# Turning the sums over the keys in blocks of 32 by 32 on VectorE

## The reference

```python
scores = jnp.clip(jnp.einsum('bhqd,bhkd->bhqk', Q, K), -80.0, 80.0)     # Q, K: 8 + 4 rotary dimensions
scores = jnp.where(causal, scores, -jnp.inf)
weights = jax.nn.softmax(scores / jnp.sqrt(jnp.float32(d_qk)), axis=-1)  # d_qk = 12
attn = jnp.einsum('bhqk,bhkd->bhqd', weights, V)
attn = attn.transpose(0, 2, 1, 3).reshape(B, S, N_HEADS * D_H)
x = _layernorm(x + attn @ W_O, axis=-1)
```

## Time and profile before

| | |
|---|---|
| time, median of 3 runs | 467.28 us (465.78 to 469.02) |
| time of the profiled execution | 468.31 us |
| its span | 466.6 us |
| mean granted TensorE clock | 0.978 |

### The profile page before, as it was taken

How to read it: one execution, slowest core, us unless ns; L and a number is a source line. 1 busy time by engine, 2 the same in 40 slices (tenths; PEclk the granted TensorE clock), 3 DMA queues, 4 the chain that set the end, 5 groups by cost and what they waited for, 6 DMA issues and landing times. The chain is left out here.

```text
span 466.6 us, 12398 instructions
## 1 busy us (share of the span) xinstructions
PE 430.2 (92%) x4259; PEld 233.6 (50%) x4259; DVE 370.6 (79%) x838; ACT 348.1 (75%) x548; POOL 166.9 (36%) x165
## 2 busy tenths in 40 slices
PE   7899999999999999999999999997999899699980
PEld 5543443434344344344443443443444798599970
DVE  4598789989896988989799889999888388366670
ACT  0697887988779888887988988787987554466650
POOL 8112112106315211431512115322002566688882
PEclk9999999999999999999999999998999899899995
DMA  3746647845442570156118305443410356577710
GB/s 100 193 124 147 156 122 152 205 128 126 102 94 68 131 162 6 42 119 138 46 35 187 77 1 136 91 99 89 115 25 1 93 145 165 156 185 212 196 55 6
DMA packets 33181, 51.67 MB, mean 111 GB/s; under 512 B 5675, under 2 KB 16337, under 8 KB 33120
## 3 DMA queue, kind: packets, MB, share of 16 engines
q1 hardware_dynamic: 25504, 37.04, 34.0%
q10 hardware_dynamic: 5344, 9.57, 7.3%
q0 software_dynamic: 2272, 4.27, 2.7%
HBM read 20.82 MB, written 5.33 MB: 56 GB/s over the span
## 5 line engine op out<-in xcount | busy, mean ns | idle before, releaser
L950 ACT ACTIVATE prob<-ring 128x1024 f32<-128x1024 f32 x288 | 273.9, 1036 | 44.9 <-PE ring L1096 43.7
L1114 PE MATMUL o_acc<-prob,v_stat 128*32 128x512 f32 (+3 forms) x1536 | 154.5, 497 | 3.2 <-DVE prob L626 2.5
L1096 PE MATMUL ring<-queries,keys 32*128 32x512 f32 (+3 forms) x1536 | 122.5, 382 | 0.9 <-ACT prob L950 0.9
L1096 PEld LDWEIGHTS ring<-queries,keys 32*128 32x128 f32 x1536 | 66.5, 184 | 72.8 <-issue 43.2
L519 POOL CAST parts<-whole_kq 128x512 fp32r<-128x512 f32 x32 | 39.1, 1221 | 139.0 <-DVE whole_kq L594 139.0
L626 DVE SCALAR_TENSOR_TENSOR prob<-prob,mask_hi 128x1024 f32<-128x1024 f32 (+1 forms) x80 | 86.1, 1076 | 0.0
L612 DVE TENSOR_SCALAR prob<-prob 128x2048 f32<-128x2048 f32 x64 | 77.4, 1220 | 7.2 <-ACT prob L950 6.2
L1023 ACT ACTIVATE prob<-ring,b1T 128x128 f32<-128x128 f32 x156 | 44.5, 368 | 38.0 <-PE ring L1214 16.8
L625 DVE TENSOR_SCALAR prob<-prob 128x1024 f32<-128x1024 f32 (+1 forms) x80 | 63.4, 793 | 11.8 <-ACT prob L950 11.6
L527 POOL DMA_INDIRECT by_expert<-xrow,index x32 | 42.9, 1341 | 50.9 <-DVE index L721 43.1
L1114 PEld LDWEIGHTS o_acc<-prob,v_stat 128*32 128x32 f32 x1536 | 34.1, 109 | 51.2 <-issue 34.0
(11 more groups left out here) (106 smaller groups left out, 312.7 us busy)
## 6 DMA issues: line engine op xcount, KB each, us to landing
queries<-parts SPq DMA_DIRECT2D x62, 256.0 KB, 3.9
v_stat<-in_w ACTq DMA_DIRECT2D x34, 256.0 KB
keys<-parts SPq DMA_DIRECT2D x64, 128.0 KB, 2.4
queries<-by_expert SPq DMA_DIRECT2D x39, 66.0 KB
xrow<-in_x_rows SPq DMA_DIRECT2D x8, 264.0 KB, 4.2
xT<-in_x_T SPq DMA_DIRECT2D x8, 256.0 KB
v_stat<-in_w SPq DMA_DIRECT2D x5, 256.0 KB
out<-prob,queries POOLq DMA_INDIRECT x39
```

Source lines behind the costliest of these rows:

```text
L950: act.activation(prob[u % P_SLOTS][:, 2 * half:2 * half + 2, :].rearrange("p h s -> p (h s)"), slot(u, half)[:], ACT.Exp, scale=SCALE).the ...
L1096: last = pe.matmul(out[:, j % 2 * QC + off:j % 2 * QC + off + w], keys[hg][r, kt * P:(kt + 1) * P], queries[hg][r, qc, part, QC - w:QC], s ...
L1114: last = pe.matmul(o_acc[j * VW:(j + 1) * VW, QC - w:QC], v_stat[b % 2][:, hg, kt, j, :], prob[u % P_SLOTS][:, j, off:off + w], start=begi ...
```

## The change

The sums are turned on VectorE by an instruction that transposes each 32x32 block of a [128, 512] tile where it stands. Since a head's rows lie in one group of 32 partitions, the turned block has queries in partitions, and 32 columns for each run of 32 queries: 9 of one group, 9 of the other, and the rest unused. `turn_sum` reads `o_acc` itself and its end (`o_turned`) lets TensorE begin the next sum; `normalize` makes one reciprocal and one product for both groups, and behind the second pair turns the result back the same way, straight into `flipped`. The jobs `turn` and `flip`, and ScalarE's copies for them, are gone. The rows of W_O are reordered on the way in to match. The other jobs move: two projections from steps 2 and 25 to 3 and 26, one from 20 to 21, `out` from 29 to 27 and from 7 to 4, `turnx`, `gate`, `rank` from 33, 34, 35 to 31, 32, 33 and from 11, 12, 13 to 9, 11, 12. In the tail every late job stands one tile sooner.

```diff
-OWN_JOBS = {0: ("project", 2, 0), 2: ("project", 3, 0), 6: ("project", 2, 1), 8: ("project", 3, 1),
-            9: ("turn", 0, 0), 22: ("turn", 0, 1), 26: ("turn", 1, 0), 28: ("flip", 0), 29: ("out", 0),
-            33: ("turnx", 0), 34: ("gate", 0), 35: ("rank", 0)}
-LATE_JOBS = {4: ("turn", 1, 1), 5: ("flip", 1), 7: ("out", 1), 11: ("turnx", 1), 12: ("gate", 1), 13: ("rank", 1)}
+OWN_JOBS = {0: ("project", 2, 0), 3: ("project", 3, 0), 6: ("project", 2, 1), 8: ("project", 3, 1),
+            27: ("out", 0), 31: ("turnx", 0), 32: ("gate", 0), 33: ("rank", 0)}
+LATE_JOBS = {4: ("out", 1), 9: ("turnx", 1), 11: ("gate", 1), 12: ("rank", 1)}
 NEXT_JOBS = {10: ("latent", 0), 14: ("latent", 1), 15: ("v", 0), 16: ("v", 1), 18: ("project", 0, 0),
-             20: ("project", 1, 0), 23: ("project", 0, 1), 25: ("project", 1, 1)}
+             21: ("project", 1, 0), 23: ("project", 0, 1), 26: ("project", 1, 1)}
...
-TAIL_AT = {1: "turn", 2: "flip", 3: "out", 6: "turnx", 7: "gate", 8: "rank"}
-PLAN_AT = (8, 9, 10)
+TAIL_AT = {2: "out", 5: "turnx", 6: "gate", 7: "rank"}
+PLAN_AT = (7, 8, 9)
...
+            def turn_sum(k):
+
+
+                dve.wait_ge(weighted, last_unit(k) + 1)
+                dve.transpose(o_blocks[k % 2][:], o_acc[:]).then_inc(o_turned, 1)
+
             def normalize(k):
 
                 pair, qc = k // NQC % PAIRS, k % NQC
-                dve.wait_ge(turned, k + 1)
-                o = misc[:].rearrange("p (t h c) -> p t h c", h=HG, c=VW)
-                inverse = rsum[:].rearrange("p (g t h) -> p g t h", g=2, h=HG)
-                for g in range(2):
-                    last = dve.reciprocal(inverse[:, g], o[:, :, :, g * VS + DH])
-                last.then_inc(rsum_ready, 1)
+                o = o_blocks[k % 2][:].rearrange("p (n r) -> p n r", r=VW)
+                dve.wait_ge(o_turned, k + 1)
+                dve.reciprocal(rsum[:], o[:, :, DH:2 * VS:VS]).then_inc(rsum_ready, 1)
                 dve.wait_ge(rsum_ready, k + 1)
...
+                rows = attn_blocks[qc][:].rearrange("p (n r) -> p n r", r=VW)[:, :, pair * 2 * DH:(pair + 1) * 2 * DH]
+                dve.tensor_tensor(rows.rearrange("p n (g d) -> p n g d", d=DH),
+                                  o[:, :, 0:2 * VS].rearrange("p n (g c) -> p n g c", c=VS)[:, :, :, 0:DH],
+                                  rsum[:].unsqueeze(3).to_broadcast([P, QC // VW, 2, DH]), ALU.mult).then_inc(attn_ready, 1)
+                if pair == PAIRS - 1:
+                    dve.wait_ge(attn_ready, k + 1)
+                    dve.transpose(flipped[qc][:], attn_blocks[qc][:]).then_inc(attn_turned, 1)
...
             for u in range(B * UB):
                 if job_at(u // UB, u % UB):
                     before_clip(*job_at(u // UB, u % UB))
+                if sum_ended(u) is not None:
+                    turn_sum(sum_ended(u))
                 clip(u)
+                if sum_ended(u) is not None:
+                    normalize(sum_ended(u))
...
             for c in range(TILES + 2):
                 if c < TILES:
                     residual(c)
+                if c == 0:
+                    turn_sum(sums(B - 1, 1, 1))
+                    normalize(sums(B - 1, 1, 1))
...
-            def o_evac(k):
-
-                act.wait_ge(weighted, last_unit(k) + 1)
-                if k >= 2:
-                    act.wait_ge(turned, k - 1)
-                act.activation(o_sb[k % 2][:], o_acc[:], ACT.Copy).then_inc(o_out, 1)
...
-                        pe.wait_ge(o_out, k)
+                        pe.wait_ge(o_turned, k)
...
-                if kind == "turn":
-                    pe.wait_ge(o_out, i + 1)
-                    pe.wait_ge(ident_ready, 2)
-                    for t in range(QC // P):
-                        last = pe.transpose(misc[:, t * P:(t + 1) * P], o_sb[i % 2][:, t * P:(t + 1) * P], ident[:])
-                    last.then_inc(turned, 1)
-                elif kind == "flip":
-
-                    pe.wait_ge(attn_ready, sums(i // Q, 1, q) + 1)
-                    for t in range(QT):
-                        last = pe.transpose(misc[:, t * P:(t + 1) * P], attn[:, q * QT + t, :], ident[:])
-                    last.then_inc(flip_mm, 1)
-                elif kind == "out":
-                    pe.wait_ge(flip_out, i + 1)
+                if kind == "out":
+                    pe.wait_ge(attn_turned, i + 1)
...
+    rows = a["L0_attn_W_O"].reshape(PAIRS, 2, HG, DH, D).transpose(2, 0, 1, 3, 4)
+    return np.ascontiguousarray(rows.reshape(HEADS * DH, D))
```

More of the change, by code:

```diff
@@ L94, in numbered @@
     kind, *which = job
-    if kind == "turn":
-        return kind, sums(b, *which)
     return (kind, b, *which) if kind == "project" else (kind, b * NQC + which[0])
@@ L131 @@
 TAIL_JOBS = [numbered(LATE_JOBS[n], B - 1) for n in sorted(LATE_JOBS)]
-TAIL_AT = {1: "turn", 2: "flip", 3: "out", 6: "turnx", 7: "gate", 8: "rank"}
-PLAN_AT = (8, 9, 10)
+TAIL_AT = {2: "out", 5: "turnx", 6: "gate", 7: "rank"}
+PLAN_AT = (7, 8, 9)
 EARLY_PLAN_AT = (B - 1) * UB + 16
-ROUTE_AT = {9: (0, 1), 10: (2, 3)}
-PAD_AT = 9
+ROUTE_AT = {8: (0, 1), 9: (2, 3)}
+PAD_AT = 8
 PADS_ACT = 2
@@ L218, in build @@
         prob = [sb(f"prob{i}", [P, HG, QC]) for i in range(P_SLOTS)]
-        o_sb = [sb(f"o_sb{i}", [P, QC]) for i in range(2)]
-        rsum = sb("rsum", [P, 2 * QC // P * HG])
-        attn = sb("attn", [P, NKT, D])
+        o_blocks = [sb(f"o_blocks{i}", [P, QC]) for i in range(2)]
+        rsum = sb("rsum", [P, QC // VW, 2])
+        attn_blocks = [sb(f"attn_blocks{i}", [P, QC]) for i in range(NQC)]
         xrow = [sb(f"xrow{i}", [P, QT, ROW]) for i in range(Q)]
@@ L300, in build @@
         scored, exped, clipped, weighted = sem("scored"), sem("exped"), sem("clipped"), sem("weighted")
-        o_out, turned, rsum_ready, attn_ready = sem("o_out"), sem("turned"), sem("rsum_ready"), sem("attn_ready")
-        flip_mm, flip_out, out_mm = sem("flip_mm"), sem("flip_out"), sem("out_mm")
+        o_turned, rsum_ready, attn_ready = sem("o_turned"), sem("rsum_ready"), sem("attn_ready")
+        attn_turned, out_mm = sem("attn_turned"), sem("out_mm")
         x_rows_in = [sem(f"x_rows_in{i}") for i in range(Q)]
@@ L336, in taken @@
             i = which[0]
-            return {"turn": (attn_ready, i + 1), "flip": (flip_out, i + 1), "out": (added, i + 1),
+            return {"out": (added, i + 1),
                     "turnx": (turnx_out, i + 1), "gate": (logits_out, i + 1), "rank": (carried, i + 2),
@@ L354, in sums_of, with sum_ended @@
             return sums(u // UB, u // NU % PAIRS, UNITS[u % NU][0])
+        def sum_ended(u):
+            return sums_of(u - LAG) if u >= LAG and last_unit(sums_of(u - LAG)) == u - LAG else None
         def last_unit(k):
@@ L723, in job @@
             def job(kind, i):
-                if kind == "turn":
-                    normalize(i)
                 if kind == "out":
@@ L742, in before_clip @@
                     turn_queries(*which)
-                if kind == "turn":
-                    normalize(*which)
                 if kind == "out":
@@ L974, in job @@
                     v_evac(i)
-                if kind == "flip":
-                    act.wait_ge(flip_mm, i + 1)
-                    act.activation(flipped[i % Q][:], misc[:], ACT.Copy).then_inc(flip_out, 1)
                 if kind == "turnx":
@@ L990, in _ @@
                 exp(u, 1)
-                if u >= LAG and last_unit(sums_of(u - LAG)) == u - LAG:
-                    o_evac(sums_of(u - LAG))
                 if job_at(u // UB, u % UB):
@@ L1032, in _ @@
                 relu(c)
-                if c == 0:
-                    o_evac(sums(B - 1, 1, 1))
                 if c + 2 < TILES:
@@ L1150, in job @@
                     pe.wait_ge(normed, i + 1)
+                    pe.wait_ge(ident_ready, 2)
                     for t in range(QT):
@@ L1299, in key_query_weights, with output_weights @@
     return out
+def output_weights(a):
+    rows = a["L0_attn_W_O"].reshape(PAIRS, 2, HG, DH, D).transpose(2, 0, 1, 3, 4)
+    return np.ascontiguousarray(rows.reshape(HEADS * DH, D))
 def constants():
@@ L1339 @@
         "w_latent": latent_weights(a), "w_kq": key_query_weights(a), "W_UV": a["L0_attn_W_UV"],
-        "W_O": a["L0_attn_W_O"],
+        "W_O": output_weights(a),
         "gate_w_T": np.ascontiguousarray(a["L0_ffn_gate_w"].T),
```

9 lines of the change are left out of this document (removed).

## The result

The changed kernel took 475.7 us as the median of 4 runs (471.5 to 479.4), against 466.8 us of the kernel before on the same chip (4 runs, 465.8 to 469.0). The ratio is 1.015, with a 95% interval from 1.011 to 1.019: slower by 7 us or so (the ratio leaves out the run of 479.4, which lay 1.7% above the fastest; the median of the other three is 473.8). The forecast was 470 with a range of 459 to 480. The profiled execution of the changed kernel took 477.65 us with a span of 475.9; the one before had 468.31 and 466.6.

What follows compares the result with a forecast made beforehand. TensorE was taken as the bound, with 1 us of slack in a half against VectorE's 5. Terms 0.3 + 1.1 + 2 x 2.0 + 0.5 - 0.7 - 2.9 gave +2.3 us on 468.31 profiled, so a median of 470, range 459 to 480.

Steps and rivals of the forecast that it cites:

- slower by over 1%: Whole kernel: chance 0.34 of a slowdown over 1%, against 0.43 for within 1% and 0.23 for faster by over 1%.
- The transpose: VectorE's new 128x512 transposes, 16 out of PSUM and 8 in SBUF: 0.65 us each from start to start.
- B: VectorE's transpose is slow, 1.2 us for four-byte elements: 11.5 us more in all, 481 us; chance 0.15.
- C: VectorE's transpose takes 0.4 us: some 5 us less than the forecast, 465 us; chance 0.12.
- The waits at o_acc: TensorE's next sum waits for VectorE's turn of the last: 1.35, 1.6, 1.35, 0.75 us at steps 2, 7, 20, 25.
- Rival A: TensorE's freed time survives: half of the o_turned stalls and the extra turnx wait go, 458 us; chance 0.2.
- The turn of x: Second half, turnx moved from step 33 to 31: wait for the layer norm becomes 1.5 us, 1.1 more.
- The halves: Middle batches cut at steps 0 and 17: first half 43.57 to 44.05 us, second 43.27 to 44.75.
- Batch 3 up to the tail: Last batch: first half +0.5 us; second half, without projections, -0.7.
- The tail: Turn, flip and the flip's wait of 2.04 go, VectorE turning the last sum in idle time: -2.9 us.
- Rival D: Routing or code loading bounds the tail's start and takes back the 2.9 us: 473 us; chance 0.13.
- TensorE's down some 16: TensorE's busy time over the whole kernel: claimed to fall by some 16 us.

Runs made afterwards that it cites:

- run 1: Changed kernel with the kept jobs (projections, out, turnx, gate, rank) at their places of before; 464.2 us against 465.1, ratio 0.998.
- run 8: Changed kernel with out, turnx, gate and rank at their former places, projections at the changed kernel's places; 473.7 us, ratio 1.013.
- run 3: Changed kernel with ScalarE's copy of o_acc kept and the jobs at their former places; 470.2 us, ratio 1.008.
- run 6: Run 5 with VectorE's transpose of the sum also ahead of the evacuation of the step's projection; 473.3 us, ratio 1.010.
- run 11: Kernel before with one idle 128x512 VectorE transpose behind each of its 16 normalizations; 469.6 us against 467.2, ratio 1.006.
- run 9: Run 1 without the turn back, which changes what it computes; 469.9 us, ratio 1.007.
- run 7: Run 1 with each turn back made twice, 0.63 us more VectorE work in a half; 470.0 us, ratio 1.005.
- run 10: Run 1 with VectorE's turn first and the lower part behind it at steps 20 and 25 alone, batch 3's early plan at step 14; 466.1 us, ratio 0.998.
- run 12: Run 10 with sooner latents, second-half turnx, gate, rank one step later, turn first at step 7, early plan at 15; 463.9 us, ratio 0.995, output off 6.5%.
- run 2: Changed kernel with ScalarE's copy of o_acc kept, jobs at the new places; 472.0 us, ratio 1.017.
- run 4: Changed kernel with a projection's lower part behind VectorE's transpose where a sum ends, jobs at the new places; 466.1 us, ratio 1.003.
- run 5: Run 1 with a projection's lower part behind VectorE's transpose where a sum ends; 467.2 us, ratio 1.000.

## Why the prediction was right, and where it was off

The mechanism held, TensorE's waits for VectorE's queue, and so did the sign of every term but batch 3's. Point by point:

- **Time.** 475.7 lies in the range, 5.7 above the forecast of 470 (the median of 473.8 lies 3.8 above it). The range was 21 us wide, so the hit says less than the terms do. The point forecast was low, and "slower by over 1%" was given 0.34 where 0.43 went to "within 1%".
- **The transpose.** 0.65 from start to start was taken, 0.63 was measured (709 ns long). Rivals B and C fell with that. The estimate of 0.71 worked out from a figure of the Trainium skill (VectorE: DVE Perf Modes, "The three transpose paths") agrees with the row to 0.01.
- **The waits at o_acc.** Forecast 1.35, 1.6, 1.35 and 0.75 for steps 2, 7, 20 and 25; measured 1.54, 1.47, 1.54 and 0.93. Rival A, which had half of them gone, fell: the order of VectorE's queue at these steps decides, not its share of busy time.
- **The turn of x.** Forecast a wait of 1.5, measured 1.62.
- **The halves.** First: 44.05 forecast, 44.2 measured. Second: 44.75 forecast, 45.24 measured; the terms at steps 20, 25 and for the turn of x were each 0.1 to 0.2 too small. Over batches 0 to 2 at the full clock that is 1.8 us: 0.6, 0.6 (batch 1) and 0.6 (batch 2).
- **Batch 3 up to the tail.** Forecast -0.2 in all, measured +0.8: behind the early plan TensorE waits 2.18 for a transpose in a step where the kernel before had no such wait, which the sum had priced at 0.75. The clock is no part of this: it falls for 3.4 us here in both kernels. (The terms of batch 3's second half also add up to -0.6, where the sum took -0.7.)
- **The tail.** -2.9 forecast, -3.1 measured; out came with no wait. Rival D fell. That the two agree so well is in part luck: the kernel before also lost some 1.7 us to the clock behind the flip's wait, which the sum did not know of; something else in the tail took about as much back, and what it was is not shown.
- **What the sum left out.** The clock. Every term was priced at 2.4 GHz. In the profiled execution 4.4 us of the 9.3 (3.0 in batch 2 and 1.4 at the start) are TensorE's work at 1.2 GHz. The 3.0 stand behind a wait that the prediction had itself named; the 1.4 stand behind none. "TensorE's down some 16" was wrong (6.9) for this reason in part; the rest is that its busy time fell by 1.2 to 1.4 us in a half at the full clock, less than the 2 us of the instructions that went.

So what failed is a step of the sum, not the mechanism: it added waits as if each cost its own length, with nothing for the clock. Forecast +2.3, measured +9.3 in the profiled pair: 4.4 clock (3.0 of them behind a wait), 1.8 mis-sized waits in the middle batches, 1.0 in batch 3, less 0.2 in the tail.

What the experiments add is which part of the diff the loss belongs to. The prediction costed the moved jobs in with the turns and did not ask what they cost apart. The new wait at o_acc is paid for by the freed turns and flips and by the tail when the jobs stay (run 1, 0.998). The loss in the second halves is the turn of x at step 31 and the projections at 21 and 26 (runs 1 and 8); to this come the clock drops, whose cause no run shows. Where the wait is taken away by another order (runs 3 and 6), another takes its place, at the turn of x above all. That this is a matter of the queue up to one point, and not of VectorE's total, is shown by run 11 (one step grew, the other half not at all); run 9 (less load, no gain) fits it.

Open: the step of 2.2 us in runs 7 and 9; why the 12 runs of run 10 don't show what its profile does; and the cause of the clock's fall as such, since the same wait was followed by it in some batches and not in others, and no run set the wait alone. Open is also why the tail of run 1 is some 3 us shorter than that of the changed kernel, with the same late jobs at the same tiles.

## What to carry to other kernels

When work moves from TensorE to an engine with idle time, list for each instruction that TensorE then waits for what that engine has queued ahead of it; this gave four waits to within 0.2 us, where VectorE's busy share (79%) and its "5 us of slack" in a half would have promised a gain. Test the freed slots apart from the move: here the new home of the work was neutral on balance and the rearranged job table cost 1.7%. A reordering that removes a wait is worth only what the waiting chain up to the engine's next deadline leaves of it, so look at that deadline first (run 12, whose output is wrong, shortened the first half by 0.65 us with a later deadline, sooner latents and an earlier turn together; which of them did it is not shown).

## What the runs showed of the hardware

- **The clock behind waits.** In batches 0 to 2 TensorE's granted clock fell from 2.4 to 1.2 GHz only in kernels in which it had waited 1.6 us or more at one place: behind 1.62 in the changed kernel (one batch of three), 1.65 in run 2, 1.67 in run 4, 1.77 in run 8, 1.81 in run 6 and 2.26 in run 3. The profiles of the kernel before and of runs 1, 5, 7, 9, 10, 11 and 12, whose longest waits there go up to 1.49, show none. The six kernels with a drop had 19 such waits in these batches, and 7 of the waits had a drop behind them. So the wait alone does not tell a drop, and elsewhere one came without it: at 16 us the changed kernel and runs 5 and 8 show one with no wait over 0.6 us in the ten before it, and in batch 3 run 10 waited 1.68 and 1.62 us without one. A drop here lasts 3.4 or 6.8 us, several matmuls, and costs 1.4 to 3 us.
- **VectorE's 32x32 transposes of f32.** 128x512 takes 709 ns out of PSUM and 711 ns in SBUF, 0.63 from start to start: 3% more than a two-source instruction of that size (687 ns).
- **A strided reciprocal.** 128x32 elements, read with a stride out of SBUF, took 346 ns; the one of 128x16 out of PSUM 221. So one instruction over twice the columns took 1.6 times as long, and less than the two that it replaced.
